# Half of the pair-product units computed with the batch on the partitions, their sums over 64 made by VectorE and ScalarE instead of TensorE

## The chip, the cores and the metric

The kernel runs on one core of a Trainium2 chip. The metric is the time of one execution on the device in microseconds (us); of several executions the median is given.

## What is computed

A batch of 1024 rows looks up one vector of 64 numbers in each of 32 tables. For each of the 496 pairs of fields (i, j) there is a 64 x 64 matrix, and the result for a pair is p K q. The 496 results and 16 dense numbers go through three layers. All is float32.

```python
p = emb_inputs[:, ROW_IDX]
q = emb_inputs[:, COL_IDX]
z = jnp.einsum('bne,hne,bnh->bn', p, kernel, q)      # 496 pairs
h = jnp.concatenate([z, dense_ctx], axis=1)          # 512 wide
h = jnp.maximum(h @ W_top1 + b_top1, 0.0)            # 512
h = jnp.maximum(h @ W_top2 + b_top2, 0.0)            # 256
y = h @ W_top3
```

## The kernel before

The batch goes through in four chunks of 256 rows. In a chunk the 32 fields stand in eight quads of four fields. GpSimd gathers a quad by eight indirect DMAs (L252), TensorE transposes it (L359) into a PSUM pair of banks, and ScalarE copies it to `emb` (L272), where the embedding lies on the partitions (two fields at a time, 64 partitions each) and the batch on the free axis.

A chunk has 64 units; quad k opens 2k+1 of them: one "inner" unit (pairs within the quad) and 2k that pair a couple of the quad's fields with two earlier couples. For a unit, TensorE multiplies stored 64x128 blocks of K by a field's 64x256 columns (L390, four matmuls, two at a time on the two halves of its rows), which gives K q for eight pairs in a 128x1024 area of PSUM. VectorE multiplies that by the other fields' `emb` (L333) into `prod`; an inner unit takes three smaller products (L325, L327, L329). The sum over the 64 embedding numbers now runs over partitions, so TensorE makes it: `reduce_batch` (L394 to L414) multiplies by a 0/1 selector, two matmuls of 512 columns a unit, four at a time on four strips of columns, and adds the rows of z into the single bank `z_ps`. It does so for eight units together, 16 matmuls. ScalarE copies `z_ps` out after every 32 units (L278).

The head of a chunk is four pieces of TensorE work on `side_ps` (L426 twice, L432, L438), put between units 5, 9, 13 and 17 of the next chunk; ScalarE applies bias and ReLU (L286, L290, L293). The last chunk's head comes at the end.

The order of each engine is the order in the code, and semaphores join them. TensorE writes units and transposed quads into a ring of three PSUM areas (`BIL_RING`), so a unit can start only when VectorE has multiplied the unit three places earlier in the ring (`wait_banks`), or ScalarE has copied the quad there. `prod` is a ring of 12 units (`PROD_RING`), freed by the reductions; `gathered` is a ring of six quads. ScalarE's program goes unit by unit as well: at unit u it stands ready to copy the quads transposed at u, and then for what else is due there.

Of the kernel before, what the change touches and what calls it, by code (L numbers as in the profile page):

```python
# [10 lines left out]
ACT = mybir.ActivationFunctionType  # L11

# [3 lines left out]
WIDTHS = [256, 256, 256, 256]  # L16
CHUNKS = len(WIDTHS)
FROM = [sum(WIDTHS[:q]) for q in range(CHUNKS)]
CHUNK = max(WIDTHS)
# [5 lines left out]
BANK = 512  # L25


def unit_list():


    units = []
    for k in range(QUADS):
        units.append((k, None, None))
        for m in (2 * k, 2 * k + 1):
            units += [(k, m, 2 * cp) for cp in range(k)]
    return units
# [5 lines left out]
FIRST_OF = [k * k for k in range(QUADS)]  # L42

BIL_RING, PROD_RING, IN_RING, GATHER_RING = 3, 12, 4, 6
BATCH_UNITS = 8
BATCHES = NUNIT // BATCH_UNITS
GROUP_BATCHES = 32 // BATCH_UNITS
BANKS = 2
GROUPS = 2 * BANKS
REDUCE_LAG = 2  # L50
SEL_WIDTH = 30 + 32
K_DMA = 8


def block_list():


    blocks = [[], []]
    for k, m, c in UNITS:
# [16 lines left out]
def slot_row(slot):  # L76
    s = slot % 64
    return slot // 64, 32 * (s % 4) + 2 * (s // 4)


def z_row(b, side):

    s, n = divmod(b, 2 * NU)
    u, i = divmod(n, 2)
    if UNITS[u][1] is not None:
        bank, row = slot_row(2 * u + s)
        return 2 * bank + i, row + side
    if i == 1 and side != s:
        bank, row = slot_row(2 * u + 1)
        return 2 * bank, row + side  # L90

    bank, row = slot_row(2 * u)
    return 2 * bank + (s if i == 0 else 0), row + (side if i == 0 else s)
# [7 lines left out]
def dense_of(k, side):  # L101
    bank, row = slot_row(2 * FIRST_OF[k] + 1)
    return FREE_ROWS.index((2 * bank + 1, row + side))
# [8 lines left out]
def transpose_unit(n):  # L112
    q, k = divmod(n, QUADS)
    first = q * NU + FIRST_OF[k]
    return max(first - 3, q * NU + FIRST_OF[k - 1] + 1) if k else max(first - 3, 0)

# [4 lines left out]
PIECES = ["l1a", "l1b", "l2", "l3"]  # L121
PIECE_UNITS = [5, 9, 13, 17]
HEAD_AT = {(q + 1) * NU + u: (q, i) for q in range(CHUNKS - 1) for i, u in enumerate(PIECE_UNITS)}


# [8 lines left out]
def interaction_tower(nc, ids, tables, dense_rows, k_blocks, w1, b1, w2, b2, w3, ident, selector, y):  # L134
    ctx = ExitStack()
    with ctx:
# [17 lines left out]
        k_sb = sb("k_sb", [P, 2 * NU, P])  # L154
        gathered = sb("gathered", [P, GATHER_RING, CHUNK // P, 2 * P])
        emb = sb("emb", [P, 2, COUPLES, CHUNK])
        prod = sb("prod", [P, PROD_RING, 2, BANK])
        inner = sb("inner", [P, IN_RING, 2, CHUNK])
        z_sb = sb("z_sb", [P, BANKS, BANK])
# [12 lines left out]
        quad_gathered = [sem(f"quad_gathered{i}") for i in range(GATHER_RING)]  # L172
# [4 lines left out]
        batch_reduced = sem("batch_reduced")  # L177
        inner_cleared = sem("inner_cleared")
# [8 lines left out]
        def gathered_count(n):  # L187
            return 16 * 4 * sum(WIDTHS[i // QUADS] // P for i in range(n % GATHER_RING, n + 1, GATHER_RING))

        def batch_of(unit):  # L190
            return unit // BATCH_UNITS

        def inner_unit(n):
            q, k = divmod(n, QUADS)
            return q * NU + FIRST_OF[k]

        @block.sync
        def _(sp):
            sp.dma_start(ids_sb[:, :, :], ids.rearrange("(p t) f -> p t f", p=P)).then_inc(ids_loaded, 16)

            def load_k(k):
                for first in range(2 * k * k, 2 * (k + 1) * (k + 1), K_DMA):
                    last = min(first + K_DMA, 2 * (k + 1) * (k + 1))
                    for s in range(2):
                        sp.dma_start(k_sb[s * EMBED:(s + 1) * EMBED, first:last, :].rearrange("p n h -> p (n h)"),
                                     k_blocks[:, (s * 2 * NU + first) * P:(s * 2 * NU + last) * P])\
                          .then_inc(k_loaded[k], 16)

            def place_dense(n):
# [4 lines left out]
                else:  # L214
                    sp.wait_ge(batch_reduced, batch_of(inner_unit(n - IN_RING)) + 1)
                for s in range(2):
                    sp.dma_start(inner[s * EMBED:s * EMBED + 1, n % IN_RING, 1, 0:WIDTHS[q]],
                                 dense_rows[dense_of(k, s):dense_of(k, s) + 1, FROM[q]:FROM[q] + WIDTHS[q]])\
# [19 lines left out]
            sp.wait_ge(head_kept, CHUNKS * (MT1 + MT2 + 1))  # L238
# [4 lines left out]
        def _(pool):  # L243
            pool.wait_ge(ids_loaded, 16)
            for n in range(NQUAD):
                q, k = divmod(n, QUADS)
                if n >= GATHER_RING:
                    pool.wait_ge(quad_transposed, n - GATHER_RING + 1)
                for f in range(4):
                    for t in range(WIDTHS[q] // P):  # L250
                        field = 4 * k + f
                        pool.indirect_dma_start(  # L252
                            gathered[:, n % GATHER_RING, t, f * EMBED:(f + 1) * EMBED], None, tables[field],
                            bass.IndirectOffsetOnAxis(ap=ids_sb[:, FROM[q] // P + t, field:field + 1], axis=0),
                        ).then_inc(quad_gathered[n % GATHER_RING], 16)

        @block.scalar
        def _(act):
            def keep_quad(n):
                q, k = divmod(n, QUADS)  # L260
                act.wait_ge(quad_transposed, n + 1)
                if q >= 2:
                    act.wait_ge(unit_multiplied, (q - 1) * NU)
                w = WIDTHS[q]

                banks = bil[BANKS_OF["quad", n]][:, :, 0:w].rearrange("p s (x b) -> p x s b", b=EMBED)
                if w == CHUNK:
                    out = emb[:, q % 2, 2 * k:2 * k + 2, :].rearrange("p c b -> p (c b)")
                    out = out.rearrange("p (x s b) -> p x s b", s=2, b=EMBED)
                else:  # L270
                    out = emb[:, q % 2, 2 * k:2 * k + 2, 0:w].rearrange("p c (s b) -> p c s b", s=2)
                act.activation(out, banks, ACT.Copy).then_inc(emb_kept, 1)  # L272

            def copy_z(q, g):
                act.wait_ge(batch_reduced, (q * BANKS + g + 1) * GROUP_BATCHES)
                if q:
                    act.wait_ge(head_done, (q - 1) * len(PIECES) + 2)
                act.activation(z_sb[:, g, 0:2 * WIDTHS[q]], z_ps[:, 0:2 * WIDTHS[q]], ACT.Copy).then_inc(z_copied, 1)  # L278

            def keep_head(q, i, banks):  # L280
                act.wait_ge(head_done, q * len(PIECES) + i + 1)
                w = WIDTHS[q]
                if PIECES[i] in ("l1a", "l1b"):
                    for j in range(2):
                        n = 2 * i + j
                        act.activation(h1_sb[:, n, 0:w], banks[:, j * w:(j + 1) * w], ACT.Relu,  # L286
                                       bias=b1_sb[:, n:n + 1]).then_inc(head_kept, 1)
                elif PIECES[i] == "l2":
                    for n in range(MT2):
                        act.activation(h2_sb[:, n, 0:w], banks[:, n * w:(n + 1) * w], ACT.Relu,  # L290
                                       bias=b2_sb[:, n:n + 1]).then_inc(head_kept, 1)
                else:
                    act.activation(y_sb[:, FROM[q] // P:(FROM[q] + w) // P], banks[:, 0:w // P], ACT.Copy).then_inc(head_kept, 1)  # L293

            for u in range(NUNIT):
                for n in TRANSPOSED_AT[u]:
                    keep_quad(n)
                if u == min(HEAD_AT):
# [3 lines left out]
                done = u - REDUCE_LAG  # L302
                if done >= 0 and (done + 1) % (BATCH_UNITS * GROUP_BATCHES) == 0:
                    copy_z(done // NU, done % NU // (BATCH_UNITS * GROUP_BATCHES))
            copy_z(CHUNKS - 1, BANKS - 1)
            for i in range(len(PIECES)):
# [3 lines left out]
        def _(dve):  # L310
            dve.memset(inner[:, :, 1, :], 0.0).then_inc(inner_cleared, 1)
            for u in range(NUNIT):
                q, (k, m, c) = u // NU, UNITS[u % NU]
                w = WIDTHS[q]
                x_y, e = bil[BANKS_OF["unit", u]], emb[:, q % 2, :, 0:w]
                out = prod[:, u % PROD_RING, :, 0:2 * w]
                dve.wait_ge(unit_done, u + 1)
                if u >= PROD_RING:
                    dve.wait_ge(batch_reduced, batch_of(u - PROD_RING) + 1)
                if m is None:  # L320
                    n = q * QUADS + k
                    a, b = 2 * k, 2 * k + 1
                    if n >= IN_RING:
                        dve.wait_ge(batch_reduced, batch_of(inner_unit(n - IN_RING)) + 1)
                    dve.tensor_tensor(out[:, 0, :].rearrange("p (j b) -> p j b", j=2), x_y[:, :, 0:w],  # L325
                                      e[:, a:a + 1, :].to_broadcast([P, 2, w]), ALU.mult)
                    dve.tensor_tensor(inner[EMBED:P, n % IN_RING, 0, 0:w], x_y[EMBED:P, 0, w:2 * w],  # L327
                                      e[EMBED:P, b, :], ALU.mult)
                    dve.tensor_tensor(inner[0:EMBED, n % IN_RING, 0, 0:w], x_y[0:EMBED, 1, w:2 * w],  # L329
                                      e[0:EMBED, a, :], ALU.mult).then_inc(unit_multiplied, 1)  # L330
                elif w == CHUNK:
                    both = e[:, c:c + 2, :].rearrange("p c b -> p (c b)").unsqueeze(1)
                    dve.tensor_tensor(out, x_y[:, :, :], both.to_broadcast([P, 2, BANK]), ALU.mult)\  # L333
                       .then_inc(unit_multiplied, 1)
                else:
                    both = e[:, c:c + 2, :].unsqueeze(1)
                    dve.tensor_tensor(out.rearrange("p j (c b) -> p j c b", c=2),
                                      x_y[:, :, 0:2 * w].rearrange("p j (c b) -> p j c b", c=2),
                                      both.to_broadcast([P, 2, 2, w]), ALU.mult).then_inc(unit_multiplied, 1)
# [178 lines left out]
```

## Time and profile before

| | |
|---|---|
| median of 3 runs | 486.28 us (486.17 to 489.33) |
| the profiled execution, device time | 487.89 us |
| its span in the trace | 486.1 us |
| TensorE busy | 429.2 us |
| VectorE busy | 306.3 us |
| ScalarE busy | 35.3 us |
| GpSimd busy | 242.0 us |
| TensorE's granted clock over the span | 0.995 of full |

Busy times are sums over the span in which at least one instruction of the engine runs. A float32 matmul stands in the trace as two records, so a unit of four matmuls is "x8" and a reduction of 16 is "x32". The start of a record in the chain of waits is where the chain passes through, and its length the time that the chain spends there.

### The profile page before, as it was taken

How to read it: one execution, taken by the hardware profiler on the slowest of the kernel's cores; microseconds unless marked ns; L12 is line 12 of the kernel's file. 1: busy time of each engine (PE TensorE's matmuls, PEld its weight loads, DVE VectorE, ACT ScalarE, POOL GpSimd, SP SyncE). 2: the span in 40 equal slices, each digit the busy share in tenths (PEclk: the TensorE clock that was granted, in tenths of full speed). 3: DMA queues.
4: the chain of work that ended last, by engine and by line, in shares of the span. 5: the costliest groups of instructions: out<-in, count | busy, mean ns of one | idle time of the engine just before them, and what ended most of it. 6: DMA issues, size and time to landing. Idle time of an engine off the chain costs nothing.

```text
span 486.1 us, 8241 instructions
## 1 busy us (share of the span) xinstructions
PE 429.2 (88%) x3552; PEld 273.3 (56%) x3552; DVE 306.3 (63%) x321; ACT 35.3 (7%) x69; POOL 242.0 (50%) x260
## 2 busy tenths in 40 slices
PE   0225999999999999999999999999999999999976
PEld 0114665555566765555566766555566766555545
DVE  0114687777777367777776367777776367777730
ACT  1000000000011100000011100000011100000002
POOL 5777777777777777736077776506074000000000
PEclk9999899999999999999999999999999999999999
DMA  5787851111111111101011111001011000000000
GB/s 126 165 173 172 197 159 28 27 27 28 27 27 28 28 26 29 29 16 24 2 26 28 28 27 29 18 6 23 2 26 21 1 2 1 1 0 1 1 1 0
DMA packets 13620, 19.20 MB, mean 39 GB/s; under 512 B 5584, under 2 KB 6928, under 8 KB 13584
## 3 DMA queue, kind: packets, MB, share of 16 engines
q1 hardware_dynamic: 5392, 10.27, 9.1%
q0 software_dynamic: 8192, 8.40, 8.8%
q8 instruction: 28, 0.46, 0.4%
q14 instruction: 8, 0.07, 0.0%
HBM read 18.65 MB, written 0.00 MB: 38 GB/s over the span
## 4 chain that ended last, share of the span: by engine, by line
PE 69%; issue 12%; DVE 9%; POOL 6%; DMA 2%; ACT 1%; DVEq 0%
PE bil L390 35%; PE z_ps L412 24%; DVE prod L333 8%; POOL gathered L252 6%; PE side_ps L426 5%; PE side_ps L432 2%; PE bil L426 1%; DMA gathered<-in_tbl,ids_sb 1%; PE bil L359 1%; PE bil L432 1%; PE side_ps L438 1%; DMA ids_sb<-in_ids 0%; ACT emb L272 0%; DVE inner L329 0%; DVE inner L327 0%
## 5 line engine op out<-in xcount | busy, mean ns | idle before, releaser
L333 DVE TENSOR_TENSOR prod<-bil,emb 128x1024 f32<-128x1024 f32 x224 | 259.8, 1216 | 129.6 <-PE bil L390 127.6
L252 POOL DMA_INDIRECT gathered<-in_tbl,ids_sb x256 | 241.8, 944 | 129.3 <-issue 75.6
L390 PE MATMUL bil<-emb,k_sb 64*128 64x256 f32 x2048 | 257.4, 395 | 15.2 <-DVE prod L333 10.3
L390 PEld LDWEIGHTS bil<-emb,k_sb 64*128 64x128 f32 x2048 | 191.8, 191 | 79.3 <-DVE prod L333 32.7
L412 PE MATMUL z_ps<-prod,sel_sb 128*32 128x512 f32 x960 | 116.5, 595 | 2.3 <-DVE prod L333 2.3
L412 PEld LDWEIGHTS z_ps<-prod,sel_sb 128*32 128x32 f32 x960 | 30.0, 110 | 70.8 <-issue 59.7
L359 PE MATMUL bil<-ident_sb,gathered 64*128 64x64 f32 x256 | 15.2, 241 | 34.7 <-DMA gathered<-in_tbl,ids_sb 34.3
L272 ACT ACTIVATE emb<-bil 128x512 f32<-128x512 f32 x32 | 19.1, 596 | 287.7 <-PE bil L359 287.7
L325 DVE TENSOR_TENSOR prod<-bil,emb 128x512 f32<-128x512 f32 x32 | 21.8, 682 | 27.9 <-PE bil L390 27.9
L359 PEld LDWEIGHTS bil<-ident_sb,gathered 64*128 64x128 f32 x256 | 12.6, 147 | 44.8 <-issue 26.4
L412 PE MATMUL z_ps<-inner,sel_sb 128*32 128x512 f32 x64 | 29.1, 602 | 0.0
L426 PE MATMUL side_ps<-z_sb,w_sb 128*128 128x256 f32 x96 | 22.3, 386 | 0.0
L426 PEld LDWEIGHTS side_ps<-z_sb,w_sb 128*128 128x128 f32 x96 | 17.8, 190 | 5.6 <-issue 3.5
L327 DVE TENSOR_TENSOR inner<-bil,emb 64x256 f32<-64x256 f32 x32 | 13.7, 427 | 0.4
L329 DVE TENSOR_TENSOR inner<-bil,emb 64x256 f32<-64x256 f32 x32 | 13.3, 417 | 0.4
L432 PE MATMUL side_ps<-h_sb,w_sb 128*128 128x256 f32 x48 | 11.2, 386 | 0.0
L432 PEld LDWEIGHTS side_ps<-h_sb,w_sb 128*128 128x128 f32 x48 | 8.9, 190 | 2.1 <-issue 1.0
L278 ACT ACTIVATE z_sb<-z_ps 128x512 f32<-128x512 f32 x8 | 4.8, 597 | 64.3 <-PE z_ps L412 64.3
L286 ACT ACTIVATE h_sb<-side_ps,b_sb 128x256 f32<-128x256 f32 x12 | 5.0, 470 | 48.7 <-PE side_ps L426 48.7
L426 PE MATMUL bil<-z_sb,w_sb 128*128 128x256 f32 x32 | 7.1, 382 | 0.8 <-ACT z_sb L278 0.8
L426 PEld LDWEIGHTS bil<-z_sb,w_sb 128*128 128x128 f32 x32 | 6.0, 190 | 2.4 <-issue 1.7
L412 PEld LDWEIGHTS z_ps<-inner,sel_sb 128*32 128x32 f32 x64 | 4.6, 109 | 0.0
(17 smaller groups left out, 23.1 us busy)
## 6 DMA issues: line engine op xcount, KB each, us to landing
k_sb<-in_k_blocks SPq DMA_DIRECT2D x24, 256.0 KB, 5.1
gathered<-in_tbl,ids_sb POOLq DMA_INDIRECT x256, 2.5
k_sb<-in_k_blocks SPq DMA_DIRECT2D x8, 192.0 KB, 6.3
inner<-in_dense_rows SPq DMA_DIRECT2D x64, 1.0 KB
w_sb<-in_w SPq DMA_DIRECT2D x1, 1024.0 KB
k_sb<-in_k_blocks SPq DMA_DIRECT2D x8, 64.0 KB, 4.9
w_sb<-in_w SPq DMA_DIRECT2D x1, 512.0 KB
ids_sb<-in_ids SPq DMA_DIRECT2D x1, 128.0 KB, 2.2
```

Source lines behind the costliest of these rows:

```text
L252: pool.indirect_dma_start(gathered[:, n % GATHER_RING, t, f * EMBED:(f + 1) * EMBED], None, tables[field], bass.IndirectOffsetOnAxis(ap=id ...
L272: act.activation(out, banks, ACT.Copy).then_inc(emb_kept, 1)
L286: act.activation(h1_sb[:, n, 0:w], banks[:, j * w:(j + 1) * w], ACT.Relu, bias=b1_sb[:, n:n + 1]).then_inc(head_kept, 1)
L325: dve.tensor_tensor(out[:, 0, :].rearrange("p (j b) -> p j b", j=2), x_y[:, :, 0:w], e[:, a:a + 1, :].to_broadcast([P, 2, w]), ALU.mult)
L327: dve.tensor_tensor(inner[EMBED:P, n % IN_RING, 0, 0:w], x_y[EMBED:P, 0, w:2 * w], e[EMBED:P, b, :], ALU.mult)
L329: dve.tensor_tensor(inner[0:EMBED, n % IN_RING, 0, 0:w], x_y[0:EMBED, 1, w:2 * w], e[0:EMBED, a, :], ALU.mult).then_inc(unit_multiplied, 1)
L333: dve.tensor_tensor(out, x_y[:, :, :], both.to_broadcast([P, 2, BANK]), ALU.mult)\
L359: last = pe.transpose(bil[BANKS_OF["quad", n]][:, s, at:at + EMBED], gathered[rows, n % GATHER_RING, t, c * P:(c + 1) * P], ident_sb[rows, ...
L390: last = pe.matmul(out[:, s, i * w:(i + 1) * w], k_sb[rows, n, :], e[rows, j, :], start=True, stop=True)
L412: last = pe.matmul(out, sel_sb[:, 30 - r:62 - r], moving, start=r == 0, stop=r == 30, tile_position=(0, 32 * col))
L426: last = pe.matmul(bank[:, j * w:(j + 1) * w], w1_sb[:, g, n * P:(n + 1) * P], z_rows(q, g), start=g == 0, stop=g == GROUPS - 1)
L432: last = pe.matmul(bank[:, n * w:(n + 1) * w], w2_sb[:, g, n * P:(n + 1) * P], h1_sb[:, g, 0:w], start=g == 0, stop=g == MT1 - 1)
```

## The change

About half of the units, 32 of the 64 in a chunk, become "batch" units. Two units that use the same field couple and adjacent K blocks, for 256 rows of the batch, are replaced by two units of 128 rows each, for 16 pairs: the stationary operand is now the field's 64x128 batch columns and the moving one 512 columns of K (L490), so that the result has the batch on the partitions and 16 pairs x 64 on the free axis. VectorE multiplies it by the gathered rows as they came (L405), no longer by `emb`, into `rows_prod`, a ring of four. The sum over 64 now runs along the free axis. For every second batch unit VectorE makes it with one `tensor_reduce` of 128x16x64 (L444), issued behind the next unit's product; for the others ScalarE makes it with 16 activations of 128x64 with an accumulator output (L349), issued two units later. The sums lie in `z_rows` with the batch on the partitions, and a new first piece of the head, "turn", transposes them on TensorE (four of 128x128, L535) and ScalarE copies them (L361).

The other 32 units (8 inner, 24 "fields") go as before, but `prod` has 6 places, reductions take 4 units each, three units after the last of them, and `z_ps` is copied once a chunk. The head's pieces stand directly behind reductions. `gathered` now holds two whole chunks, quads are transposed four units ahead instead of three, and K's blocks are the same in size and in the order of loading.

```diff
+BATCH_PAIRS = [0, 0, 2, 2, 2, 3, 3, 4]
+VECTOR_SUMS = {v for v in range(NB) if v % 2 == 1}
-BIL_RING, PROD_RING, IN_RING, GATHER_RING = 3, 12, 4, 6
-BATCH_UNITS = 8
-REDUCE_LAG = 2
+BIL_RING, PROD_RING, ROWS_RING, IN_RING = 3, 6, 4, 4
+BATCH_UNITS = 4
+REDUCE_LAG = 3
+SUM_LAG = 2
...
+            def sum_rows(u):
+                act.wait_ge(unit_multiplied, u + 1)
...
+                for x in range(16):
+                    row = rows_prod[:, v % ROWS_RING, x, :]
+                    last = act.activation(row, row, ACT.Copy, accum_out=z_rows[:, q % 2, t, col + x:col + x + 1])
+                last.then_inc(scalar_summed, 1)
...
             for u in range(NUNIT):
                 for n in TRANSPOSED_AT[u]:
                     keep_quad(n)
+                if u >= SUM_LAG and UNITS[(u - SUM_LAG) % NU][0] == "batch":
+                    sum_rows(u - SUM_LAG)
...
+                if kind == "batch":
+                    v = batched_before(u)
+                    if v >= ROWS_RING:
+                        free_rows(v - ROWS_RING)
+                    row = gathered[:, q % 2, t, 2 * c * EMBED:(2 * c + 8) * EMBED].unsqueeze(1)
+                    dve.tensor_tensor(rows_prod[:, v % ROWS_RING, :, :].rearrange("p (j x) h -> p j (x h)", j=2),
+                                      x_y[:, :, :], row.to_broadcast([P, 2, BANK]), ALU.mult).then_inc(unit_multiplied, 1)
+                    return
...
+                dve.tensor_reduce(z_rows[:, q % 2, t, col:col + 16], rows_prod[:, v % ROWS_RING, :, :], AXIS.X, ALU.add)\
+                   .then_inc(vector_summed, 1)
...
+                if kind == "batch":
+                    for s in range(2):
+                        rows = slice(s * EMBED, (s + 1) * EMBED)
+                        last = pe.matmul(out[:, s, :], e[rows, m, t * P:(t + 1) * P],
+                                         k_sb[rows, 2 * part:2 * part + 4, :].rearrange("p n h -> p (n h)"),
+                                         start=True, stop=True)
...
+                if PIECES[i] == "turn":
+                    pe.wait_ge(scalar_summed, (q + 1) * NA)
+                    pe.wait_ge(vector_summed, (q + 1) * NV)
+                    for g in range(2):
+                        for t in range(CT):
+                            at = (g * CT + t) * P
+                            last = pe.transpose(bank[:, at:at + P], z_rows[:, q % 2, t, g * P:(g + 1) * P],
+                                                ident_sb[:, :])
```

On TensorE, around the head's second piece (`side_ps` from `z_sb` and `w_sb`) in the second chunk, before:

```order
L412 MATMUL z_ps<-inner,sel_sb 32x512
L412 MATMUL z_ps<-prod,sel_sb 32x512 x6
L426 MATMUL side_ps<-z_sb,w_sb 128x256 x8
L390 MATMUL bil<-emb,k_sb 128x256 x12
L359 MATMUL bil<-ident_sb,gathered 128x64 x8
L390 MATMUL bil<-emb,k_sb 128x256 x4
L432 MATMUL side_ps<-h_sb,w_sb 128x256 x8
```

and now, where a batch unit is two matmuls of 512 columns (`bil` from `k_sb` and `emb`):

```order
L524 MATMUL z_ps<-inner,sel_sb 32x512
L524 MATMUL z_ps<-prod,sel_sb 32x512 x6
L542 MATMUL side_ps<-z_sb,w_sb 128x256 x8
L490 MATMUL bil<-k_sb,emb 128x512 x6
L505 MATMUL bil<-emb,k_sb 128x256 x4
L490 MATMUL bil<-k_sb,emb 128x512 x2
L505 MATMUL bil<-emb,k_sb 128x256 x4
L473 MATMUL bil<-ident_sb,gathered 128x64 x8
```

A reduction ahead of a head piece is eight matmuls in place of sixteen, and half of the units are of the new form. On VectorE, in a stretch of quads 4 and 5 of the first chunk, before:

```order
L333 TENSOR_TENSOR prod<-bil,emb 128x1024 x8
L325 TENSOR_TENSOR prod<-bil,emb 128x512
L327 TENSOR_TENSOR inner<-bil,emb 64x256
L329 TENSOR_TENSOR inner<-bil,emb 64x256
L333 TENSOR_TENSOR prod<-bil,emb 128x1024 x10
```

and now, in the same part of the program:

```order
L405 TENSOR_TENSOR rows_prod<-bil,gathered 128x1024
L414 TENSOR_TENSOR prod<-bil,emb 128x1024
L405 TENSOR_TENSOR rows_prod<-bil,gathered 128x1024
L414 TENSOR_TENSOR prod<-bil,emb 128x1024
L444 TENSOR_REDUCE z_rows<-rows_prod 128x16
L421 TENSOR_TENSOR prod<-bil,emb 128x512
L423 TENSOR_TENSOR inner<-bil,emb 64x256
L425 TENSOR_TENSOR inner<-bil,emb 64x256
```

The products are as many and as large as they were, and a reduction (its output is 128x16, its input 128x16x64) stands behind every fourth unit or so. On ScalarE, in the second chunk, before:

```order
L278 ACTIVATE z_sb<-z_ps 128x512
L272 ACTIVATE emb<-bil 128x512
L286 ACTIVATE h_sb<-side_ps,b_sb 128x256 x2
L272 ACTIVATE emb<-bil 128x512
L286 ACTIVATE h_sb<-side_ps,b_sb 128x256 x2
```

and now:

```order
L361 ACTIVATE z_sb<-side_ps 128x512
L349 ACTIVATE rows_prod,z_rows<-rows_prod 128x64 x32
L336 ACTIVATE emb<-bil 128x512
L349 ACTIVATE rows_prod,z_rows<-rows_prod 128x64 x32
L365 ACTIVATE h_sb<-side_ps,b_sb 128x256 x2
L349 ACTIVATE rows_prod,z_rows<-rows_prod 128x64 x16
L336 ACTIVATE emb<-bil 128x512
```

The copies of quads to `emb` and of the head's results now stand behind groups of 16, 32 or more small activations on the same engine.

## Rows read from the trace of the kernel before

**Rows 1.** The page, part 1: busy us, share of the span, instructions.

```profile
PE 429.2 (88%) x3552; PEld 273.3 (56%) x3552; DVE 306.3 (63%) x321; ACT 35.3 (7%) x69; POOL 242.0 (50%) x260
```

**Rows 2.** Busy time by stretch: start:end, length, PE, PEld, DVE, ACT, POOL, clock.

```profile
0.00:131.10 131.10, 92.63 (x762) 57.47 (x764) 70.49 (x75) 6.66 (x10) 97.02 (x107) 0.99 0.46 104
131.10:240.30 109.20, 105.39 (x891) 67.16 (x890) 76.32 (x80) 8.44 (x17) 69.44 (x74) 1.00 0.12 24
```

**Rows 3.** Groups, stretch 131.1 to 240.3, VectorE: busy us, mean ns | idle before.

```profile
L333 DVE TENSOR_TENSOR prod<-bil,emb 128x1024 f32<-128x1024 f32 x56 | 65.0, 1215 | 32.7 <-PE bil L390 32.2
L325 DVE TENSOR_TENSOR prod<-bil,emb 128x512 f32<-128x512 f32 x8 | 5.4, 681 | 0.0
```

**Rows 4.** The chain of waits, in order of time: start us, us, what.

```profile
118.35 8.05 PE bil L390 x64
126.40 3.64 PE z_ps L412 x32
...
182.99 0.04 issue
183.03 3.99 PE bil L390 x32
187.02 3.57 PE z_ps L412 x32
...
227.58 8.05 PE bil L390 x64
```

**Rows 5.** Timeline of TensorE from 142 us: start us, us, what.

```profile
143.41 3.67 PE L390 MATMUL bil<-emb,k_sb 64*128 64x256 f32 x32
147.02 3.72 PE L426 MATMUL side_ps<-z_sb,w_sb 128*128 128x256 f32 x16
150.67 0.46 PE L359 MATMUL bil<-ident_sb,gathered 64*128 64x64 f32 x8
```

**Rows 6.** Timeline of VectorE from 118 and from 142 us.

```profile
119.46 9.14 DVE L333 TENSOR_TENSOR prod<-bil,emb 128x1024 f32<-128x1024 f32 x8 [2.54 <-PE bil L390]
...
146.82 0.68 DVE L325 TENSOR_TENSOR prod<-bil,emb 128x512 f32<-128x512 f32 x1
...
148.30 1.21 DVE L333 TENSOR_TENSOR prod<-bil,emb 128x1024 f32<-128x1024 f32 x1
```

**Rows 7.** Timeline of ScalarE from 142 us.

```profile
143.25 0.60 ACT L278 ACTIVATE z_sb<-z_ps 128x512 f32<-128x512 f32 x1 [4.83 <-PE z_ps L412]
143.75 0.59 ACT L272 ACTIVATE emb<-bil 128x512 f32<-128x512 f32 x1
```

**Rows 8.** Groups of the whole span, ScalarE: busy us, mean ns | idle before.

```profile
L278 ACT ACTIVATE z_sb<-z_ps 128x512 f32<-128x512 f32 x8 | 4.8, 597 | 64.3 <-PE z_ps L412 64.3
...
L293 ACT ACTIVATE y_sb<-side_ps 128x2 f32<-128x2 f32 x3 | 0.5, 172 | 22.1 <-PE side_ps L438 22.1
```

**Rows 9.** Timeline of all engines at the start and at the end.

```profile
48.27 0.69 PE L359 MATMUL bil<-ident_sb,gathered 64*128 64x64 f32 x8 [3.06 <-DMA gathered<-in_tbl,ids_sb]
...
457.67 5.86 PE L390 MATMUL bil<-emb,k_sb 64*128 64x256 f32 x48
458.85 6.88 DVE L333 TENSOR_TENSOR prod<-bil,emb 128x1024 f32<-128x1024 f32 x6 [2.55 <-PE bil L390]
465.78 3.64 PE L412 MATMUL z_ps<-prod,sel_sb 128*32 128x512 f32 x32 [2.26 <-DVE prod L333]
484.04 0.17 ACT L293 ACTIVATE y_sb<-bil 128x2 f32<-128x2 f32 x1 [1.14 <-PE bil L438]
```

**Rows 10.** Who waited for whom: engine line <- releaser: us, times, longest.

```profile
DVE prod L333 <- PE bil L390: 127.6, 40, 8.4
PE bil L359 <- DMA gathered<-in_tbl,ids_sb: 34.3, 4, 18.5
PE bil L390 <- DVE prod L333: 10.3, 19, 0.6
```

More of the change, by code:

```diff
@@ L15 @@
 HIDDEN1, HIDDEN2 = 512, 256
[L16 to L19, printed above, removed]
+CHUNK = 256
+CHUNKS = BATCH // CHUNK
+CT = CHUNK // P
 TILES = BATCH // P
@@ L25, with part_list @@
 BANK = 512
+GROUPS = 4
+def part_list():
+    parts = []
+    for k in range(QUADS):
+        parts.append((k, None, None))
+        for m in (2 * k, 2 * k + 1):
+            parts += [(k, m, 2 * cp) for cp in range(k)]
+    return parts
+PARTS = part_list()
+NPART = len(PARTS)
+BATCH_PAIRS = [0, 0, 2, 2, 2, 3, 3, 4]
 def unit_list():
@@ L32, in unit_list @@
     for k in range(QUADS):
-        units.append((k, None, None))
-        for m in (2 * k, 2 * k + 1):
-            units += [(k, m, 2 * cp) for cp in range(k)]
+        own = [n for n in range(NPART) if PARTS[n][0] == k]
+        units.append(("inner", own[0], 0))
+        couples = [(x, m) for x in range(0, k - 1, 2) for m in range(2)][:BATCH_PAIRS[k]]
+        firsts = [own[1 + m * k + x] for x, m in couples]
+        batch = [("batch", n, t) for n in firsts for t in range(CT)]
+        fields = [("fields", n, 0) for n in own[1:] if n not in firsts and n - 1 not in firsts]
+        while batch or fields:
+            if len(batch) >= len(fields):
+                units.append(batch.pop(0))
+            else:
+                units.append(fields.pop(0))
     return units
@@ L76, in slot_row @@
 def slot_row(slot):
-    s = slot % 64
-    return slot // 64, 32 * (s % 4) + 2 * (s // 4)
+    return 32 * (slot % 4) + 2 * (slot // 4)
 def z_row(b, side):
[L83 to L87, printed above, removed]
+    s, n = divmod(b, 2 * NPART)
+    part, i = divmod(n, 2)
+    for first in (part, part - 1):
+        if first in FIRST_PARTS:
+            at = 16 * FIRST_PARTS.index(first) + 8 * s + 4 * (part - first) + 2 * i + side
+            return 2 + at // P, at % P
+    u = [v for v in range(NU) if UNITS[v][:2] in (("inner", part), ("fields", part))][0]
+    a = summed_before(u)
+    if UNITS[u][0] == "fields":
+        return i, slot_row(2 * a + s) + side
     if i == 1 and side != s:
[L89 to L93, printed above, removed]
+        return 0, slot_row(2 * a + 1) + side
+    return (s, slot_row(2 * a) + side) if i == 0 else (0, slot_row(2 * a) + s)
 FREE_ROWS = sorted({(g, r) for g in range(GROUPS) for r in range(P)}
@@ L185, in interaction_tower, with inner_batch @@
         block = ctx.enter_context(nc.Block())
[L187 to L193, printed above, removed]
+        def inner_batch(n):
             q, k = divmod(n, QUADS)
-            return q * NU + FIRST_OF[k]
+            return summed_before(q * NU + FIRST_OF[k]) // BATCH_UNITS
         @block.sync
@@ L261, in keep_quad @@
                 act.wait_ge(quad_transposed, n + 1)
-                if q >= 2:
+                if q >= 2 and k == 0:
                     act.wait_ge(unit_multiplied, (q - 1) * NU)
[L264 to L271, printed above, removed]
@@ L272, in keep_quad @@
-                act.activation(out, banks, ACT.Copy).then_inc(emb_kept, 1)
-            def copy_z(q, g):
-                act.wait_ge(batch_reduced, (q * BANKS + g + 1) * GROUP_BATCHES)
+                banks = bil[BANKS_OF["quad", n]][:, :, 0:CHUNK].rearrange("p s (x b) -> p x s b", b=EMBED)
+                out = emb[:, q % 2, 2 * k:2 * k + 2, :].rearrange("p c b -> p (c b)")
+                out = out.rearrange("p (x s b) -> p x s b", s=2, b=EMBED)
+                act.activation(out, banks, ACT.Copy).then_inc(emb_kept, 1)
@@ L301, in _ @@
                     keep_head(*HEAD_AT[u], side_ps)
[L302 to L306, printed above, removed]
+            for u in range(NUNIT - SUM_LAG, NUNIT):
+                if UNITS[u % NU][0] == "batch":
+                    sum_rows(u)
+            keep_head(CHUNKS - 1, 0, side_ps)
+            copy_z(CHUNKS - 1)
+            for i in range(1, len(PIECES)):
                 keep_head(CHUNKS - 1, i, bil[i % BIL_RING][:, 0, :])
@@ L310, in _ @@
         def _(dve):
[L311 to L316, printed above, removed]
-                dve.wait_ge(unit_done, u + 1)
[L318 to L331, printed above, removed]
@@ new lines, in multiply @@
+            def multiply(u):
+                q, (kind, part, t) = u // NU, UNITS[u % NU]
+                k, m, c = PARTS[part]
+                x_y, e = bil[BANKS_OF["unit", u]], emb[:, q % 2, :, :]
+                dve.wait_ge(unit_done, u + 1)
+                if kind == "batch":
+                    v = batched_before(u)
+                    if v >= ROWS_RING:
[3 more added lines that the diff above has]
+                                      x_y[:, :, :], row.to_broadcast([P, 2, BANK]), ALU.mult).then_inc(unit_multiplied, 1)
+                    return
+                a = summed_before(u)
+                out = prod[:, a % PROD_RING, :, :]
+                if a >= PROD_RING:
+                    dve.wait_ge(batch_reduced, (a - PROD_RING) // BATCH_UNITS + 1)
+                if kind == "fields":
@@ L400, in reduce_batch @@
+                for a in range(b * BATCH_UNITS, (b + 1) * BATCH_UNITS):
+                    u = unit_at(a)
+                    q, (kind, part, _) = u // NU, UNITS[u % NU]
                     for i in range(2):
-                        slot = 2 * (u % NU) + i
-                        _, row = slot_row(slot)
+                        row = slot_row(2 * (a % NS) + i)
                         col, r = row // 32, row % 32
-                        moving = prod[:, u % PROD_RING, i, 0:2 * WIDTHS[q]]
@@ L405, in reduce_batch @@
-                        if m is None and i == 1:
-                            n = q * QUADS + k
+                        moving = prod[:, a % PROD_RING, i, :]
+                        if kind == "inner" and i == 1:
+                            n = q * QUADS + PARTS[part][0]
                             pe.wait_ge(dense_placed[n % IN_RING], 32 * (n // IN_RING + 1))
-                            moving = inner[:, n % IN_RING, :, 0:WIDTHS[q]]
-                        out = z_ps[32 * col:32 * (col + 1), 0:2 * WIDTHS[q]]
@@ L410, in reduce_batch @@
-                        if m is None and i == 1:
-                            out = out.rearrange("p (h b) -> p h b", h=2)
-                        last = pe.matmul(out, sel_sb[:, 30 - r:62 - r], moving,
+                            moving = inner[:, n % IN_RING, :, :].rearrange("p h b -> p (h b)")
+                        last = pe.matmul(z_ps[32 * col:32 * (col + 1), :], sel_sb[:, 30 - r:62 - r], moving,
                                          start=r == 0, stop=r == 30, tile_position=(0, 32 * col))
```

223 lines of the change are left out of this document (139 added, 84 removed).

## The prediction

> **What bounds the kernel now.** I read the busy shares first [rows 1]: TensorE 429.2 us of 486.1, VectorE 306.3, ScalarE 35.3. TensorE looks like the bound, but a share is an average, so I took one chunk alone. The chain of waits shows the same pattern once a chunk, 118.35 and 227.58 being the same place: a period of 109.2 us [rows 4]. In it TensorE is busy 105.4 us and VectorE 76.3 [rows 2], and VectorE's 32.7 idle us before its products end with TensorE's `bil` [rows 3]. So VectorE starves in steps. Where TensorE is away on a reduction of eight units (16 matmuls, 3.57 us, [rows 4]) or on a head piece (3.65 us from 147.02 to 150.67, [rows 5]), VectorE has at most the three units of the PSUM ring in hand; the next product comes 1.18 us after the next unit begins (457.67 to 458.85, [rows 9]). When it has work again, TensorE is held by the ring instead: its eight units at 118.35 take 8.05 us for the chain [rows 4], where unheld units go at 3.61/4 = 0.90 us (143.41 to 147.02, [rows 5]). Both engines share the path, by turns.
>
> Outside the repeating part the start waits for the gathers (quad 3 comes at 48.27, [rows 9]; 34.3 us of such waits in all, [rows 10]), and the tail from VectorE's last product (458.85 + 6.88 = 465.73) to the end is 20.4 us [rows 9].
>
> **The durations.** A product of 128x1024: eight in a row take 9.14 us and the record of one is 1.21, so the pitch is (9.14 - 1.21)/7 = 1.133 us [rows 6]. An inner unit: 146.82 to 148.30, 1.48 us [rows 6]. A reduction of 16 matmuls is four rounds of four: 3.57/4 = 0.89 us a round of 512 columns [rows 4].
>
> **What is removed.** 32 units of 64 per chunk need no selector matmuls: four of eight reductions of 3.57 us, 14.3 us per chunk, 57 us in all. A reduction of four units is two rounds, 1.8 us, and there are eight per chunk.
>
> **The batch units on TensorE.** Two matmuls of 512 columns side by side in place of four of 256. The trace has none of this form; the nearest row is the round of the reduction, 0.89 us, and the unit now is 0.90. I take 0.89. Were it 1.0, the whole kernel would be 3.5 us longer (below), a small term. The "turn": a head piece is eight matmuls of 256 columns in 3.65 us, 0.46 each [rows 5]; at 128 columns four take between 0.9 and 1.8, and I take 1.05. TensorE's work per chunk falls by about 13 us.
>
> **The sums on VectorE.** All 64 products a chunk stay. Sixteen sums of 1024 elements come in addition. No row shows this instruction. Per element a product costs (1215 - 681)/512 = 1.04 ns [rows 3], and a sum reads as many elements, so the nearest row is the product itself: 1.133 us. I take it. Above, without the overlap of 0.08 us between neighbours, 1.22; below, if an instruction with a single input went two elements a cycle, about 0.6. So VectorE's work per chunk is 56 x 1.133 + 8 x 1.48 + 16 x 1.133 = 63.5 + 11.8 + 18.1 = 93.4 us.
>
> The Trainium skill, "VectorE: DVE Perf Modes", perf-mode tier table, gives `tensor_reduce` the single rate only and calls it the slowest operation of the engine. By it the low end falls away, and the sum stays what it is.
>
> **The sums on ScalarE.** Sixteen activations of 128x64 a group, sixteen groups a chunk. A plain activation: 172 ns for two elements, 597 for 512, so 425/510 = 0.83 ns an element, and 172 + 62 x 0.83 = 223 ns for 64 [rows 8]. Neighbours overlap: from 143.25 to 143.75 is a pitch of 0.50 us [rows 7] for a record of 597 ns, 97 less. That gives 0.126 us each and 2.0 us a group, if the accumulator's output is free. The trace has no accumulator output, and I can't exclude that it costs an instruction of its own. The cheapest here is 172 ns, 75 of them beside an overlap. If it overlaps as neighbours do, 0.126 + 0.075 = 0.20 and a group 3.2 us; if it has to wait for its activation's end, 0.22 + 0.075 = 0.30 and 4.8 us; with no overlap at all 0.395 and 6.3 us. I take 0.20 to 0.25, the lower half, because in the rows nothing on ScalarE waits for its neighbour's end, and keep the rest for the range. Per chunk that is 256 x 0.20 + about 7 for the copies = 58 us of some 109: no bound by itself.
>
> The Trainium skill, "VectorE: DVE Perf Modes", section on the TRN2 errata, speaks against the change here: instructions that read SBUF pay a fixed cost each, and it advises tiles of 512 or more elements. The row of 172 ns for two elements [rows 8] agrees that most of a 64-element activation is fixed cost.
>
> **The sum.** I laid both programs out, engine by engine in their order, with these durations and their semaphores; for the kernel before this gives a chunk of 109.3 us (109.2 in the trace). For the changed one, per chunk: VectorE's work of 93.4 and idle places for which TensorE is away. At a head piece behind a reduction TensorE is gone for 1.8 + 3.65 us; from the start of its last unit it is 0.89 + 5.45 + 1.18 = 7.5 us to the next product, and the ring holds three units and one sum, 3 x 1.133 + 1.133 = 4.5, or 4.9 with an inner unit: 2.6 to 3.0 us idle. The layout has 2.9, 2.9 and 4.0 at the three large pieces, 2.8 at the turn, 2.0 where `z_ps` is cleared for a new chunk, and 0.7 in small ones: 15.3. So 93.4 + 15.3 = 108.7 us, in place of 109.3. What TensorE gives up (13 us) doesn't come back, since VectorE gets 18 us more and the three-area ring still starves it at the head.
>
> The first chunk ends at the same time within 0.1 us: the gathers set its start, and the saving is again used by sums. GpSimd's order is the same, and it now runs ahead further, which nothing waits for. Three chunks: 3 x 0.6 = 1.9 less (unrounded). The tail: last reduction 3.6 becomes a vector sum 1.1, the turn 1.2 (with its restart) and a reduction 1.8, 0.5 more. Span: 486.1 - 1.9 + 0.5 = 484.7 us. The median of the runs shown lies 0.2 above the span (486.28), so 484.9.
>
> Where ScalarE's group costs more, a copy of a quad to `emb` stands behind it on the same engine, and so do the copies for the head. TensorE needs the copy's PSUM area again two units later and `emb` for its next inner unit, and VectorE then has two products and a sum in hand, 3 x 1.133 = 3.4 us. A group up to about 3.6 us is hidden. The layout gives for a group of 3.7 us a span of 488.3, for 4.0 us 491, for 4.8 us 505, for 5.6 us 536 and for 6.3 us 571.
>
> I predict the middle of 484.9 (0.20 us an activation) and 491 (0.25): **488 us**.
>
> **Rivals.**
> - *ScalarE late, moderately* (0.25 to 0.32 us an activation): TensorE's units wait for `emb` copies queued behind sum groups. For it: the accumulator output is unpriced and 1024 instructions carry it. Against: an engine that is busy 8.4 us of a chunk [rows 2] has much room. 491 to 515 us.
> - *ScalarE as the bound* (over 0.32): 256 x 0.35 + 7 = 97 us a chunk, and with the groups in bursts it doesn't fit. 515 to 570 us. This and the one above end on the slower side; the point from which it decides is a group of 4.0 us.
> - *The sums on VectorE at the double rate* (0.6 us): VectorE's chunk shrinks by 8.5 us, and by the same layout the span is 460 us. Nothing in the rows speaks for it; products run at one element per 1.04 ns.
> - *VectorE's sum costs 1.22 in full*: span 489, within the likeliest case. *A batch unit of 1.0 us*: 488.
>
> **How the numbers follow.** Likeliest, VectorE and the ring as the bound with ScalarE hidden or nearly so: 0.48, its own range 484 to 491. ScalarE moderately late 0.29; ScalarE bound 0.17; cheap sums 0.06. Leaving out the cheap sums and most of the bound case gives 483 to 515. A measurement of this kernel can tell about 1% from no change, 481.4 to 491.1: faster 0.06, same 0.48, slower 0.46.
>
> **What would show it.** Right: VectorE busy about 306 + 64 x 1.13 = 378 us; TensorE busy well below 429; a chunk of about 109 us; VectorE idle some 15 us per chunk, ended by TensorE's units, at the head pieces; ScalarE's groups of 16 in 3.2 to 4.0 us. Wrong: groups over 4 us with TensorE waiting for ScalarE's `emb` copies, VectorE waiting for ScalarE's sums (the ring `rows_prod`), a batch unit far from 0.89 us, or sums far from 1.13.

## The result

The changed kernel takes 503.5 us in the median (503.08 to 504.46). Beside it the kernel before took 487.8 us, and the ratio is 1.031, interval 1.025 to 1.038: slower by 3%. The profiled execution has a span of 502.0 us against 486.1, and TensorE's granted clock fell from 0.995 to 0.942. The device time of an execution is 1.8 to 1.9 us more than its span, in these runs and in those below.

The page of the changed kernel, part 1 (busy us, share, instructions) and rows of part 2 (tenths of the clock and of busy time in 40 slices), answers to [rows 1]:

```profile
PE 409.6 (82%) x2544; PEld 216.5 (43%) x2544; DVE 376.2 (75%) x385; ACT 282.2 (56%) x2117; POOL 241.9 (48%) x260
...
PE   0225799889888899989888898989887998989866
...
DVE  0113899899968977599978977599978977599930
...
PEclk9999979899979899899989799899989799899989
```

TensorE has less work but only 20 us less busy time, since part of it ran slowly. VectorE has 376 us of work, as forecast (378). The groups of VectorE in one chunk, 269.37 to 381.87 us, columns as in [rows 3]:

```profile
L405 DVE TENSOR_TENSOR rows_prod<-bil,gathered 128x1024 f32<-128x1024 f32 x32 | 38.4, 1212 | 9.4 <-PE bil L490 9.3
L414 DVE TENSOR_TENSOR prod<-bil,emb 128x1024 f32<-128x1024 f32 x24 | 29.0, 1212 | 8.7 <-PE bil L505 6.1 <-PE z_ps L524 2.6
L444 DVE TENSOR_REDUCE z_rows<-rows_prod 128x16 f32<-128x1024 f32 x16 | 19.3, 1205 | 0.0
```

The chunk is 112.5 us long, where it was 109.2 [rows 4]: the same two matmuls stand in the chain of waits behind the turn of two chunks.

```profile
268.78 0.59 PE side_ps L535 x4
269.37 1.08 PE bil L490 x4
...
381.28 0.59 PE side_ps L535 x4
381.87 1.08 PE bil L490 x4
```

The period is VectorE's work plus idle time, as the prediction took it, but the idle time is 18.6 us (9.4 + 8.7 and 0.5 in small ones) and not 15.3.

ScalarE in a group of sums, timeline from 300 us: each activation is followed by a second instruction that reads the accumulator.

```profile
300.02 0.24 ACT L349 ACTIVATE rows_prod<-rows_prod 128x64 f32<-128x64 f32 x1
...
300.16 0.19 ACT L349 ACTIVATION_READ_ACCUMULATOR rows_prod<-rows_prod 128x1 f32 x1
...
300.26 0.24 ACT L349 ACTIVATE rows_prod<-rows_prod 128x64 f32<-128x64 f32 x1
```

From 300.02 to 300.26 is one pitch, 0.24 us, and 16 make a group of 3.8 us. The reads overlap their activations: the records are 241 and 187 ns, together 0.43.

What the forecast had no term for stands in TensorE's timeline from 272 us:

```profile
274.01 1.13 PE L490 MATMUL bil<-k_sb,emb 64*128 64x512 f32 x4 [1.00 <-DVE rows_prod L405]
275.57 0.46 PE L473 MATMUL bil<-ident_sb,gathered 64*128 64x64 f32 x8 [0.43 <-DVE inner L425]
277.74 2.08 PE L490 MATMUL bil<-k_sb,emb 64*128 64x512 f32 x4 [1.70 <-DVE rows_prod L405]
279.61 1.91 PE L505 MATMUL bil<-emb,k_sb 64*128 64x256 f32 x8
281.31 1.91 PE L490 MATMUL bil<-k_sb,emb 64*128 64x512 f32 x4
...
284.95 1.02 PE L490 MATMUL bil<-k_sb,emb 64*128 64x512 f32 x4
285.81 1.03 PE L505 MATMUL bil<-emb,k_sb 64*128 64x256 f32 x8
```

and the stretches around it (columns as in [rows 2]; the clock is the third number from the end):

```profile
268.00:276.00 8.00, 6.57 (x44) 2.92 (x36) 5.70 (x8) 6.59 (x52) 6.17 (x7) 1.00 0.15 30
276.00:284.00 8.00, 6.30 (x26) 3.66 (x26) 6.95 (x7) 8.00 (x66) 5.87 (x8) 0.57 0.13 27
284.00:292.00 8.00, 8.00 (x56) 5.09 (x52) 6.46 (x8) 1.75 (x15) 6.17 (x7) 1.00 0.14 29
```

TensorE waits for VectorE three times in a row, 1.00, 0.43 and 1.70 us, then runs at its lower level of 1.2 GHz: units start 1.70 us apart (279.61 to 281.31) instead of 0.86 (284.95 to 285.81). The Trainium skill, "TensorE: Matmul & The Clock Gate", section on HAM oscillation, tells of a clock that falls again and again where TensorE waits for DMAs between bursts of matmuls. The waits there are longer than the ones here; the trace shows the same fall behind waits of at most 1.70 us for another engine, 0.57 in this stretch.

### The profile page after: what moved, and what is told of

Its sections match the earlier page's. It is cut to its first block, busy times and chain, and to the rows that moved or that the text cites. A ratio compares the mean times of both kernels' runs of the same rounds, so it can differ in the third digit from the quotient of the medians.

```text
span 502.0 us, 8351 instructions
## 1 busy us (share of the span) xinstructions
PE 409.6 (82%) x2544; PEld 216.5 (43%) x2544; DVE 376.2 (75%) x385; ACT 282.2 (56%) x2117; POOL 241.9 (48%) x260
## 4 chain that ended last, share of the span: by engine, by line
PE 35%; DVE 26%; issue 23%; ACT 8%; POOL 6%; DMA 2%; DVEq 0%
DVE rows_prod L405 12%; PE bil L490 9%; PE bil L505 8%; PE z_ps L524 7%; ACT rows_prod L349 6%; POOL gathered L320 6%; DVE z_rows L444 5%; DVE prod L414 5%; PE side_ps L542 4%; PE side_ps L547 2%; DVE prod L421 2%; DVE inner L425 2%; PE bil L542 1%; DVE inner L423 1%; DMA gathered<-in_tbl,ids_sb 1%
## 5 line engine op out<-in xcount | busy, mean ns | idle before, releaser
L349 ACT ACTIVATE rows_prod<-rows_prod 128x64 f32<-128x64 f32 x1024 | 245.1, 241 | 75.4 <-DVE rows_prod L405 75.3
L349 ACT ACTIVATION_READ_ACCUMULATOR rows_prod<-rows_prod 128x1 f32 x1024 | 191.9, 187 | 0.0
L405 DVE TENSOR_TENSOR rows_prod<-bil,gathered 128x1024 f32<-128x1024 f32 x128 | 153.4, 1211 | 36.8 <-PE bil L490 36.4
L490 PE MATMUL bil<-k_sb,emb 64*128 64x512 f32 x512 | 147.8, 669 | 30.7 <-DVE rows_prod L405 17.1
L505 PE MATMUL bil<-emb,k_sb 64*128 64x256 f32 x1024 | 151.7, 424 | 9.5 <-ACT emb L336 5.6
L414 DVE TENSOR_TENSOR prod<-bil,emb 128x1024 f32<-128x1024 f32 x96 | 116.0, 1212 | 37.8 <-PE bil L505 27.9
L505 PEld LDWEIGHTS bil<-emb,k_sb 64*128 64x128 f32 x1024 | 103.1, 206 | 90.6 <-DVE rows_prod L405 37.4
L490 PEld LDWEIGHTS bil<-k_sb,emb 64*128 64x128 f32 x512 | 45.7, 200 | 73.9 <-DVE rows_prod L405 25.9
L444 DVE TENSOR_REDUCE z_rows<-rows_prod 128x16 f32<-128x1024 f32 x64 | 77.1, 1205 | 0.0
L524 PE MATMUL z_ps<-prod,sel_sb 128*32 128x512 f32 x448 | 64.7, 628 | 0.0
L336 ACT ACTIVATE emb<-bil 128x512 f32<-128x512 f32 x32 | 18.6, 582 | 57.9 <-PE bil L473 49.0
```

The lines of the kernel that those rows point to most:

```text
L349: last = act.activation(row, row, ACT.Copy, accum_out=z_rows[:, q % 2, t, col + x:col + x + 1])
L405: dve.tensor_tensor(rows_prod[:, v % ROWS_RING, :, :].rearrange("p (j x) h -> p j (x h)", j=2), x_y[:, :, :], row.to_broadcast([P, 2, BANK ...
L444: dve.tensor_reduce(z_rows[:, q % 2, t, col:col + 16], rows_prod[:, v % ROWS_RING, :, :], AXIS.X, ALU.add)\
L490: last = pe.matmul(out[:, s, :], e[rows, m, t * P:(t + 1) * P], k_sb[rows, 2 * part:2 * part + 4, :].rearrange("p n h -> p (n h)"), start= ...
L505: last = pe.matmul(out[:, s, i * CHUNK:(i + 1) * CHUNK], k_sb[rows, n, :], e[rows, j, :], start=True, stop=True)
L524: last = pe.matmul(z_ps[32 * col:32 * (col + 1), :], sel_sb[:, 30 - r:62 - r], moving, start=r == 0, stop=r == 30, tile_position=(0, 32 * ...
```

## Experiments

The "layout" in the expectations is the one of the prediction: both programs' orders with the durations of their rows, always at full clock. It is a calculation and not a run; its figures are quoted as the prediction and the expectations state them. Experiments 2, 3 and 9 leave out sums, so their kernels do not compute the whole result.

**1. Fill TensorE's waits.** Extra matmuls that nothing reads, ahead of the waits (`FILL` gives their number by unit of a chunk):

```diff
+FILL = {1: 3, 11: 2, 12: 4, 16: 1, 23: 2, 32: 2, 39: 3, 45: 1, 56: 2, 60: 1}
...
+                for _ in range(FILL[r]):
+                    pe.matmul(side_ps[:, 0:CHUNK], k_sb[:, 0, :], k_sb[:, 0:2, :].rearrange("p n h -> p (n h)"),
+                              start=True, stop=True)
```

> The changed kernel, with extra TensorE work that computes nothing of the output: at ten places in each chunk where the trace shows TensorE waiting for VectorE or ScalarE, 1 to 4 matmuls of 128x256 into the idle bank side_ps (0.45 us each, 21 a chunk, about 9.4 us of work a chunk) stand ahead of the wait. Theory (the clock): the changed kernel's span of 502.0 us is the layout's 489 us with the measured 0.239 us an activation, plus 13 us of units that run at 1.71 in place of 0.86 us after TensorE sat idle for 1 to 2 us; with the gaps filled the granted clock goes from 0.94 to near 0.99 and the span falls to 489 to 493. Rival (ScalarE and VectorE set the length, the slow units lie in slack): the clock rises but the time stays at 500 to 504. Rival (extra work only costs): 505 or more.

Measured: 495.2 us, ratio to the kernel before 1.014 (1.010 to 1.017), span 494.2, clock 0.986. More work on TensorE made the kernel 8 us faster. The same place in its timeline:

```profile
270.03 1.13 PE L491 MATMUL bil<-k_sb,emb 64*128 64x512 f32 x4
271.59 0.46 PE L474 MATMUL bil<-ident_sb,gathered 64*128 64x64 f32 x8 [0.43 <-DVE inner L426]
271.99 1.99 PE L574 MATMUL side_ps<-k_sb 128*128 128x256 f32 x8
273.91 1.13 PE L491 MATMUL bil<-k_sb,emb 64*128 64x512 f32 x4
274.89 1.13 PE L506 MATMUL bil<-emb,k_sb 64*128 64x256 f32 x8
```

The wait of 1.70 us is now four extra matmuls (L574), and the units behind it start 0.98 us apart. The clock was a cause, and worth 7.8 us of span. From 256 to 368 us it is now 1.00, and the chunk is 110.3 us (turns at 264.73 and 374.99). The span ends 1 to 5 us above what the clock theory gave, so the clock isn't all of the 13 us.

**2. Almost no work on ScalarE.** One activation a group instead of sixteen:

```diff
-                for x in range(16):
+                for x in range(1):
```

> The changed kernel with one of the sixteen activations in each ScalarE group (fifteen of sixteen of its sums are left out; z_rows is set to zero once at the start). ScalarE's group goes from 3.8 us to 0.24. Theory A (ScalarE's groups delay the copies to emb, which make TensorE idle and lower its clock): most of the loss goes, span 485 to 489. Rival (VectorE's longer queue alone makes TensorE idle, and the clock stays low): 494 to 500.

Measured: 497.6 us, ratio 1.018 (1.013 to 1.022), span 495.9, clock 0.965. Taking away 225 us of ScalarE's busy time (282.2 to 57.6) gives 6 us. The result lies in the rival's range: TensorE waits for VectorE without ScalarE's groups too, and the wait of 1.70 us ahead of low clock is there again, ending at 276.57 (the clock is 0.67 from 278 to 282).

**3. Almost no sums on VectorE.** They read 2 elements in place of 1024:

```diff
-                dve.tensor_reduce(z_rows[:, q % 2, t, col:col + 16], rows_prod[:, v % ROWS_RING, :, :], AXIS.X, ALU.add)\
+                dve.tensor_reduce(z_rows[:, q % 2, t, col:col + 1], rows_prod[:, v % ROWS_RING, 0:1, 0:2], AXIS.X, ALU.add)\
```

> The changed kernel with VectorE's sums shrunk to two elements each (their results are left out; z_rows is set to zero once at the start), so 64 x about 1.0 us of VectorE's work goes. If VectorE is the bound as predicted, the layout gives a span of 455 us at full clock, and up to 465 with some slow units. Rival (ScalarE sets the length): hardly below 490.

Measured: 456.8 us, ratio 0.937 (0.932 to 0.941), span 454.8, clock 0.992, with ScalarE's groups in full. VectorE is what sets the length: 64 sums in full cost 47 us of span, where the same number of groups on ScalarE costs 6. Both figures hold what low clock goes with the sums.

**4. The head's pieces away from the reductions.**

```diff
-HEAD_AT = {reduce_unit((q + 1) * BATCHES + i): (q, i) for q in range(CHUNKS - 1) for i in range(len(PIECES))}
+HEAD_AT = {reduce_unit((q + 1) * BATCHES + i) + 3: (q, i) for q in range(CHUNKS - 1) for i in range(len(PIECES))}
```

> The changed kernel with the head's five pieces three units later, so that none stands directly behind a reduction; TensorE is then away for 1.8 or 3.65 us at a time instead of 5.45. If the ring of three areas that runs dry is what keeps VectorE idle, the layout gives 470 us at full clock; with units at low clock up to 485. Rival (the idle places only move): 498 to 503.

Measured: 483.5 us, ratio 0.989 (0.986 to 0.993), span 482.0, clock 0.961. A shift of three units gives 20 us, and this form of the change beats the kernel before by 1%. It lies in the range for the ring that runs dry, 470 at full clock to 485. VectorE's work is the same (375.6 us busy); only its idle time went. It had starved while TensorE was away for 1.8 + 3.65 us at a stretch.

**5 and 6. The kernel before, with smaller reductions.** The theory of the ring says that the kernel before loses time in the same way. First reductions of 4 units:

```diff
-BATCH_UNITS = 8
+BATCH_UNITS = 4
-PIECE_UNITS = [5, 9, 13, 17]
+PIECE_UNITS = [7, 11, 15, 19]
```

> The kernel before, with reductions of 4 units instead of 8 (1.8 us at a time instead of 3.57, twice as often) and the head's pieces after units 7, 11, 15, 19, between reductions. Nothing is added or taken away. If VectorE's 33 us of idle time a chunk come from the ring running dry while TensorE is away, the layout gives a span of 461 us. Rival (TensorE's work of about 101 us a chunk plus change-over losses sets the length): 480 to 487.

Measured: 470.1 us, ratio 0.960 (0.956 to 0.964), span 468.6. With 2 units and [6, 10, 14, 18]:

> The same with reductions of 2 units (0.9 us, one round of four matmuls) and the head's pieces after units 6, 10, 14, 18. The layout gives 454 us, with TensorE as the bound at 102 us a chunk. Rival (each change between units and reductions costs some 0.1 to 0.2 us, and there are now 128 of them): 465 to 475.

Measured: 483.9 us, ratio 0.988 (0.983 to 0.993), span 482.9, above the layout's 454 and above the rival's range as well. The chunk is 109.4 us long, as in the kernel before (109.2); with 4 units it is 105.4. The chain of waits shows why this one is no better. Reductions of 4 units:

```profile
302.29 3.65 PE bil L390 x32
305.94 1.85 PE z_ps L412 x16
307.79 3.65 PE bil L390 x32
```

Reductions of 2 units:

```profile
302.07 1.93 PE bil L390 x16
304.00 0.99 PE z_ps L412 x8
304.99 1.93 PE bil L390 x16
```

Neither chain has a wait in these lines. Two units and their reduction take 2.92 us; at 0.90 a unit and 0.89 a round it would be 2.69, so 0.23 is lost at the two changes between the forms of matmul. With 4 units it is 5.50 against 5.38, 0.12. Times 128 and 64 reductions that is 29 and 8 us, which is what both spans lie above the layout (482.9 to 454, 468.6 to 461).

The two chains give the loss without the layout too. Two more units and one more round take 5.50 - 2.92 = 2.58 us, 0.86 each. Three times 0.86 leaves 0.34 of the 2.92, and six times 0.86 leaves 0.34 of the 5.50: the loss is the same 0.34 us for each pair of changes. It looks like 0.23 and 0.12 above, since 0.90 and 0.89 already hold a part of it.

**7. Share the sums otherwise.**

```diff
-VECTOR_SUMS = {v for v in range(NB) if v % 2 == 1}
+VECTOR_SUMS = {v for v in range(NB) if v % 4 == 1}
```

> The changed kernel with the sums shared otherwise: VectorE makes 8 of the 32 in a chunk and ScalarE 24, with the result unchanged. If VectorE alone were the bound it would gain 8 x 1.13 = 9 us a chunk, 36 in all (466). With ScalarE's group at 3.8 us and the copies to emb behind it, the layout gives 519 at full clock, more at a lower one: 515 to 540.

Measured: 534.8 us, ratio 1.093 (1.088 to 1.097), span 532.6, clock 0.923. With 24 groups a chunk ScalarE is too late. Who waited for whom on TensorE (us, times, longest):

```profile
PE bil L490 <- ACT emb L336: 32.4, 18, 4.5
PE bil L490 <- DVE rows_prod L405: 11.5, 20, 1.0
```

In the changed kernel TensorE's waits for ScalarE's copies came to 2.2 us in the chunk from 269.37. This is the rival "ScalarE late", made real: copies to `emb` queued behind groups. At 16 groups a chunk it is small, at 24 it decides.

**8. Experiments 1 and 4 together**, with 14 filling matmuls a chunk (the expectation miscounts them as 15).

> The changed kernel with both the head's pieces three units later and the waits of TensorE filled with matmuls that compute nothing of the output (15 of 128x256 a chunk, at places where that kernel's trace or layout shows waits). If low clock and the head's places are two separate losses, the gains of each alone (span 502.0 to 494.2 and to 482.0) add up: the later head alone ran at clock 0.961, so some 5 to 7 us of its 482.0 are still the clock, and the span is 475 to 477 at a clock of 0.98 or more. Rival (both remove the same loss): 480 to 483.

Measured: 477.2 us, ratio 0.974 (0.970 to 0.979), span 475.0, clock 0.989. The two losses are separate: 20 us by the place of the head, then 7 more by the clock. At full clock the later head takes the chunk from 110.3 us to 104.1.

**9. Experiments 1 and 2 together.**

> The changed kernel with one of sixteen activations in each ScalarE group (fifteen of sixteen of its sums left out, z_rows set to zero at the start) and the waits of TensorE filled as in the first experiment. Without ScalarE's groups the span was 495.9 at a clock of 0.965, with the filling alone 494.2 at 0.986. If ScalarE's own share at full clock is the layout's 3 to 4 us, this one is at 489 to 491. Rival (ScalarE's groups cost nothing but the clock): 494. Rival (their costs add without overlap): 488.

Measured: 494.4 us, ratio 1.008 (1.005 to 1.011), span 490.8, clock 0.989. Against experiment 1 the profiled spans are 3.4 us apart and the ratios 0.6%, 3 us, but the medians only 0.8 us (the spans of this one's seven runs go from 490.8 to 493.1, those of experiment 1 from 493.2 to 494.2), and the chunk is 109.6 us instead of 110.3. So ScalarE's groups cost 1 to 3 us at nearly full clock; the layout's 3 to 4 is at the upper end, and the rival that gives them nothing but the clock (494) isn't far away.

The chain of waits of the changed kernel runs through these groups all the same, for 6% of its span (30 us):

```profile
292.38 0.84 ACT h_sb L365 x2
293.22 3.81 ACT rows_prod L349 x32
297.03 0.49 ACT emb L336
```

A share of the chain is not a price: with almost no groups the span is only 6 us shorter (experiment 2).

**10. Experiment 5 with the head where it was**, directly behind reductions.

> The kernel before with reductions of 4 units and nothing else: the head's pieces stay after units 5, 9, 13, 17, which now is directly behind a reduction, as in the changed kernel. With the pieces between reductions the span was 468.6. The layout says 2 us more, 470 to 472. Rival (a head piece behind a reduction costs as much as it did in the changed kernel, where moving it gave 20 us): 480 or more.

Measured: 470.5 us, ratio 0.959 (0.954 to 0.964), span 469.4. The head behind a reduction costs nothing that can be seen here (0.5 us in the median; the chunk is 105.3 us in one and 105.4 in the other) and 20 us in the changed kernel. My reading is that the difference is who has slack: here VectorE has 77 us of work in a chunk of 105 and catches up, there 94 of 112.5, and what it loses each time it starves stays lost. No run tests this by itself.

## Why the prediction came out as it did

The bound was right, the size of the change was not. I gave 488, with 483 to 515; 503.5 lies inside by way of the slower cases, and "slower" had 0.46 against 0.48 for "same". The likeliest case, 484 to 491, was wrong. That the range holds is partly luck: its upper part stood for a ScalarE that is late, and the time came mostly by another way.

- *VectorE and the ring as the bound*: right. Taking its sums away gives 47 us (experiment 3, 454.8; the layout gave 455 for it). VectorE's busy time, 376.2, and the pitch of products and sums, 1.13 us, were right: the chunk's 93.4 us of work measured 93.8. At full clock its idle time is 16.6 us a chunk (110.3 less 93.7, experiment 1), where the prediction had 15.3.
- *The batch unit at 0.89 us*: right at full clock. The one at 284.95 leaves room for the next unit 0.86 us later. Behind other work it is longer: in the filled timeline, 273.91 to 274.89, 0.98 us after the extra matmuls. Taken as 1.0 throughout it would have been worth 3.5 us in all.
- *ScalarE's group*: the term was mis-sized. I took 0.20 to 0.25 us an activation and worked the sum with 0.20; it is 0.24, a group of 3.8 us, and the layout gives 489 for that. The rival "moderately late" set its point at 4.0 us and this group is just under it; by experiment 9 the groups cost 1 to 3 us. It was the right place for a doubt but not where the loss is. The bounds, 0.126 and 0.395, held; the read of the accumulator is an instruction of its own and overlaps. The estimate of 223 ns for a record came from activations that read PSUM [rows 8]; these read SBUF, and the record is 241 ns.
- *TensorE's clock*: missing. The step that failed is "what TensorE gives up doesn't come back": I took the idle time of TensorE as free, and every duration at full clock. Idle time isn't free: VectorE as the bound means that TensorE waits, and after a few waits of up to 1.7 us in a row it runs at half its clock, just when VectorE needs units. That is 7.8 us (experiment 1). Which wait takes the clock down, and how long one may be, no run tells. In the kernel before the longest wait for VectorE on TensorE's matmuls was 0.6 us [rows 10], and the clock stood at 1.00 in a chunk [rows 2].
- *What remains*: experiment 1 ends 4 to 5 us above the layout's 489 (spans 493.2 to 494.2), and experiment 8 5 to 7 above its 470. The cause is open. The changes between reductions and units cost more than the layout has for them (experiments 5 and 6); at 0.12 us the 32 reductions here would make 4 us of TensorE's time, an estimate, and TensorE isn't the bound. A change between the two forms of unit costs nothing (284.95 to 285.81). The clock is still low outside the chunks: in experiment 1 it is 0.55, 0.50 and 0.67 in the stretches of 4 us from 44 us, where the kernel before has 0.97, 0.60 and 1.00, and 0.79 from 472 to 480. Neither was tried alone.
- *The turn and the tail*: at 268.71 to 269.30 the turn takes 0.59 us, where I took 1.05; too small to matter.
- *From span to device time*: mis-sized. I added 0.2 us, the median of some executions less the span of another. The profiled execution took 487.89 us with a span of 486.1, 1.8 more, and 503.76 with 502.0 now. That is 1.6 us too little.

So the sum would have read: 484.7, plus 4 for the activation's true price, plus 8 for the clock, plus 5 whose cause is open, a span of 502, and 503.5 with 1.8 for the device time.

The runs also show where some of the time of the kernel before lay. The change takes 11 us a chunk from TensorE (busy 105.4 before and 94.2 in experiment 3, both at full clock) and gives 18 to VectorE, which had 33 us a chunk idle. Part of that idle time came from TensorE's absences of 3.57 us and more with three units in the ring. Halving the reductions shortens those absences without moving any work and gives 4% (experiment 5), 3.9 us of it in each repeating chunk and the rest in the start and the tail, against 2.6% for the best form of the change (experiment 8). Experiments 5 and 10 are the fastest kernels with the whole result. VectorE still idles for 28 us of a chunk of 105 there: TensorE, busy 103.7 us, is then the bound.

## What to carry to other kernels

Where two engines wait for each other by turns, look at the longest absence of the producer against what the ring holds, before moving work: shorter batches gain until the changes between forms of instruction eat it up (here at 2 units a batch). Putting them apart from other long pieces matters where the consumer has little slack (20 us in experiment 4, nothing to be seen in experiment 10). Work moved onto the engine that has idle time is only free if that idle time isn't the price of the ring. And a TensorE made idle on purpose can lose its clock, as it did here, so a saving on TensorE is to be checked against the granted clock in short stretches; filling its waits with useless matmuls shows in one run about what the clock costs.

## What was not expected of the hardware

- TensorE's clock fell in a kernel that keeps it 82% busy, and its mean of 0.942 hides stretches of 8 us at 0.57. Waits of 1.00, 0.43 and 1.70 us in a row came ahead of one; with the waits filled the same place ran at full clock.
- An activation of 128x64 with an accumulator output takes 0.24 us in a row, its two records of 241 and 187 ns overlapping; from the rows of plain activations the prediction had 0.126 us for it if the accumulator were free.
- Changing between matmuls of 64x128 stationary tiles and four-strip reductions costs 0.34 us for a pair of changes, with reductions of 8 records and of 16 alike, where a unit or a round between its like takes 0.86.
